# One attention-and-experts kernel: head sums in four column groups of TensorE, reciprocals laid as diagonal squares

## The chip, the cores and the metric

The kernel runs on one core of a Trainium2 chip. The metric is the device time of one execution in microseconds: the median of three runs is 970.37 us (966.24 to 972.15).

## The reference, cut to what matters

A layer on x of 4096 tokens by 512 channels, all in float32: linear attention with decay, a layer norm, a mixture of 64 experts with a shared one, a second layer norm. The change lies in the attention, and there in its denominator:

```python
qkv = x @ w_qkv                          # q, k, v: 16 heads of 32 channels
q, k = phi(q), phi(k)                    # phi(z) = elu(z) + 1
running_kv   = decay_scan(k * v)         # s_t = decay * s_{t-1} + x_t, per head
running_ksum = decay_scan(k)
den = clip(sum(q * running_ksum, over the 32 channels of a head), 1e-06)
out = q * running_kv / den               # den: one number per token and head
x1  = layernorm(x + out @ w_out)
```

## The kernel before, in words

**Tiling.** The tokens are cut into NB = 8 blocks of BT = 512, each into NJ = 4 tiles of 128. The channels are cut into KC = 4 chunks of 128, so a chunk holds 4 heads. In the attention, channels lie on the partitions and tokens run along the free axis. A step (it, c) projects chunk c of block it into k, v and q; there are 32 steps. To keep float32 accuracy at the higher rate, matmuls use float32r operands split into a high and a low part, three products each (`three`); an unsplit float32 matmul is recorded by the profiler as two weight loads and two matmuls.

**A step on each engine.** TensorE (`step` in the tensor block) projects k, v and q, twelve matmuls each, and between them it runs pieces of the block before, given by `mix(it, c, at)` for at = 0, 1, 2: head sums, the spreading of the reciprocals, and the rows of the output projection. ScalarE takes exp and relu of k and q out of PSUM. VectorE forms phi_k, scans it into run_k, multiplies by v into kv and scans that, forms phi_q, then qk = phi_q * run_k (one of five buffers), and one step later the numerator num = phi_q * run_kv. VectorE also splits, divides, adds the residual, takes norm statistics and routes tiles to experts.

**The denominator of a block** comes one block later, in the step c = 0:
- `sums(b, at)` on TensorE, at = 0 after the projection of k and at = 1 after that of v. For two of the four tiles each it multiplies the four chunks of qk, as the stationary operand (128 channels by 128 tokens), with `head_sum` (128 channels by 16 heads) and leaves 16 numbers per token, tokens on the partitions, in `small_ps`. The gate matmuls of the routing write into the same bank.
- `sums(b, at)` on VectorE clips them into `den` and writes the reciprocals twice into `rden`, at columns 0 and 32.
- `turn_rden(b)` on TensorE, after the projection of q: four transposes put heads on partitions and tokens along the free axis.
- `rden_high(b)` on ScalarE rounds the result to float32r, `rden_low(b)` on VectorE subtracts for the low part. Both lie in `rden_parts`, at partitions 0 to 15 and 32 to 47.
- `spread(b, part)` on TensorE, one matmul of 512 columns a chunk with `head_send` (ones where head and channel match), writes the reciprocal of every channel's head; `divide` on VectorE multiplies the numerator by it.

GpSimd builds the constants at the start (`head_sum`, `head_send` and the masks), each counted on the semaphore `consts`, and later computes the norms' scale and shift and issues the scatter of slots, one tile of six indirect DMAs a step.

**What sets the order.** All queues are written out by hand: `mix`, `sums_at`, `divide_at`, `out_at` and `tile_of` give the place of each piece, and every engine runs the same plan in order. A projection may overwrite one of three PSUM banks when the entry of `freed` says that its reader three projections before is through. After the eight blocks, the sums and the division of the last block stand in a stretch written out by itself, among the last tiles' norms, gates and counts and the first matmuls of the shared expert (`unit`):

```python
            count_rest(LAST - 5)
            sums(NB - 1, 0, LAST - 3)
            sums(NB - 1, 1, LAST - 3)
            count_before(LAST - 4)
            turn_x1(LAST - 3)
            gate(LAST - 3, 2 * NB)
            turn_rden(NB - 1)
            count_rest(LAST - 4)
            unit()
            spread(NB - 1, 0)
```

In the first block VectorE also splits the staged weights between its scans, so its queue there is longer than later. The experts follow when the table of slots is complete.

## Time and profile before

| | |
|---|---|
| median of three runs | 970.37 us (966.24 to 972.15) |
| profiled execution, span from first to last instruction | 967.4 us |
| profiled execution's own time beside its span | not listed apart |
| TensorE busy | 943.6 us, 98% |
| VectorE busy | 683.8 us, 71% |
| ScalarE busy | 502.8 us, 52% |
| GpSimd busy | 466.4 us, 48% |
| mean granted TensorE clock | 0.991 of full speed |

The attention part with its end lasts to about 490 us, the experts and the final norm fill the rest. PE is TensorE's matmuls, PEld its weight loads (they overlap), DVE VectorE, ACT ScalarE, POOL GpSimd. A busy matmul's end is modelled, and neighbours overlap; what a matmul costs is the distance to the next start. A line number is that of the helper that issues the instruction, so most matmuls show L1608 and are told apart by the names of their operands.

### The profile page before, as it was taken

To read this page: it belongs to the slowest core of one execution; us is meant where nothing else is said; L and a number is where in the kernel's file an instruction comes from. 1 tells how busy PE (TensorE), PEld (TensorE's weight loads), DVE (VectorE), ACT (ScalarE), POOL (GpSimd) and SP (SyncE) were. 2 spreads that over 40 slices of the span, in tenths; PEclk is the share of its full clock that TensorE was granted. 3 is DMA by queue.
4 is the path that set the end of the run, shared out by engine and by line. 5 is a ranking of instruction groups with operands and counts; after the bars stand their busy time and mean duration, and the time that the engine had idled before them with its cause. 6 is when DMAs were issued, how large, how long until landed. Compare 5 with 4: busy or idle time off the path is not lost. (4 is left out here: it accounts for less than half of the span.)

```text
span 967.4 us, 15236 instructions
## 1 busy us (share of the span) xinstructions
PE 943.6 (98%) x4658; PEld 757.0 (78%) x4658; DVE 683.8 (71%) x1251; ACT 502.8 (52%) x1015; POOL 466.4 (48%) x543
## 2 busy tenths in 40 slices
PE   8999999999999999999999999999999999999996
PEld 7888888888888888877887777777767777777875
DVE  7977786969778796887766565566565665636776
ACT  5532434434443443534447665566655665635775
POOL 4002264565556554587234544445545454432564
PEclk9999999999999999989999999999999999999999
DMA  6343452444252434346569999999999999979973
GB/s 202 96 145 109 144 125 91 131 114 132 80 167 91 119 109 140 103 152 231 171 195 272 292 323 307 310 318 294 327 319 316 308 318 298 320 135 372 373 268 118
DMA packets 114191, 203.93 MB, mean 211 GB/s; under 512 B 18496, under 2 KB 56384, under 8 KB 113088
## 3 DMA queue, kind: packets, MB, share of 16 engines
q1 hardware_dynamic: 93584, 159.87, 50.6%
q0 software_dynamic: 19520, 35.75, 16.3%
q10 hardware_dynamic: 1008, 7.34, 2.0%
q8 instruction: 39, 0.64, 0.3%
q14 instruction: 40, 0.33, 0.1%
HBM read 143.03 MB, written 59.88 MB: 210 GB/s over the span
## 5 line engine op out<-in xcount | busy, mean ns | idle before, releaser
L1511 POOL DMA_INDIRECT slot_table<-tokens,slot_of x162 | 179.2, 1106 | 112.0 <-issue 59.6
L1553 POOL DMA_INDIRECT acc_rows<-eo,table_sb x64 | 112.0, 1750 | 170.4 <-ACT eo L879 133.0
L1608 PE MATMUL bank<-x_hi,wqkv_hi 128*128 128x512 f32 x384 | 153.2, 399 | 1.4 <-DVE wqkv_lo L963 1.3
L1376 DVE TENSOR_TENSOR wgu_lo<-wgu,wgu_hi 128x1536 fp32r<-128x1536 f32 x64 | 112.4, 1758 | 55.0 <-ACT wgu_hi L873 55.0
L1608 PE MATMUL bank<-x_hi,wqkv_lo 128*128 128x512 f32 x384 | 150.8, 393 | 0.0
L1608 PE MATMUL bank<-x_lo,wqkv_hi 128*128 128x512 f32 x384 | 150.6, 392 | 0.0
L1608 PE MATMUL bank<-wdn,hid_et 96*128 96x512 f32 x256 | 122.1, 599 | 7.6 <-ACT hid_et L915 7.6
L873 ACT CAST wgu_hi<-wgu 128x1536 fp32r<-128x1536 f32 x64 | 94.5, 1477 | 12.5 <-DMA wgu<-w_gu 12.1
L1542 POOL DMA_INDIRECT xg<-x_rows,table_sb x64 | 74.9, 1170 | 42.0 <-DVE table_sb L1111 22.7
L1608 PE MATMUL bank<-wgu_hi,xgt_hi 128*128 128x384 f32 x256 | 91.6, 358 | 0.0
L647 ACT ACTIVATE e<-bank 128x512 f32<-128x512 f32 x64 | 38.0, 594 | 97.3 <-PE bank L1608 97.3
L1608 PE MATMUL bank<-wgu_hi,xgt_lo 128*128 128x384 f32 x256 | 86.0, 336 | 0.0
L1608 PE MATMUL bank<-wgu_lo,xgt_hi 128*128 128x384 f32 x256 | 85.9, 336 | 0.0
L1608 PEld LDWEIGHTS bank<-x_hi,wqkv_hi 128*128 128x128 f32 x384 | 72.7, 189 | 16.3 <-DVE wqkv_lo L963 2.0
L1608 PEld LDWEIGHTS bank<-x_hi,wqkv_lo 128*128 128x128 f32 x384 | 72.5, 189 | 16.0
L1608 PEld LDWEIGHTS bank<-x_lo,wqkv_hi 128*128 128x128 f32 x384 | 72.6, 189 | 14.8
L1608 PEld LDWEIGHTS bank<-wdn,hid_et 96*128 96x128 f32 x256 | 43.5, 190 | 40.2 <-issue 30.7
L1403 DVE SCALAR_TENSOR_TENSOR silu_e<-tanh_e,bank 128x192 f32<-128x192 f32 x64 | 22.6, 353 | 66.9 <-ACT tanh_e L903 66.7
L1495 POOL TENSOR_SCALAR rstd<-mv 128x1 f32<-128x1 f32 x32 | 9.2, 286 | 115.3 <-DVE mv L990 114.0
L879 ACT ACTIVATE eo<-bank,xg 128x512 f32<-128x512 f32 x64 | 44.3, 692 | 39.2 <-DMA acc_rows<-eo,table_sb 33.9
L1608 PE MATMUL bank<-wout_hi,att_hi 128*128 128x512 f32 x128 | 52.0, 407 | 1.7 <-issue 1.2
L903 ACT ACTIVATE tanh_e<-bank 128x192 f32<-128x192 f32 x64 | 21.2, 331 | 61.6 <-PE bank L1608 61.3
(179 smaller groups left out, 2211.6 us busy)
## 6 DMA issues: line engine op xcount, KB each, us to landing
wgu<-w_gu SPq DMA_DIRECT2D x64, 768.0 KB, 8.8
wdn<-w_down SPq DMA_DIRECT2D x64, 384.0 KB, 8.8
xres<-x SPq DMA_DIRECT2D x32, 256.0 KB, 3.2
x_turned<-x1t SPq DMA_DIRECT2D x32, 256.0 KB, 2.8
x_rows<-x SPq DMA_DIRECT2D x32, 256.0 KB, 3.1
acc_rows<-x SPq DMA_DIRECT2D x32, 256.0 KB, 3.1
fin<-acc_rows SPq DMA_DIRECT2D x8, 1024.0 KB, 12.1
odd<-acc_rows SPq DMA_DIRECT2D x8, 1024.0 KB, 13.5
```

The lines of the kernel that those rows point to most:

```text
L647: act.activation(e_sb[q][:, :], ps[:, :], ACT.Exp)
L873: act.copy(wgu_hi[e % 2][:, :, :], wgu_buf[e % NG][:, :, :]).then_inc(wgu_hi_done, 1)
L879: act.activation(eo[eo_slot[e]][:, :], eo_ps[:, :], ACT.Copy, scale=xg[e % NXG][:, D + e:D + e + 1]).then_inc(eo_done, 1)
L903: act.activation(tanh_e[:, :], gu_ps[e % 2][:, 0:I], ACT.Tanh, scale=0.5).then_inc(tanh_e_done, 1)
L1376: dve.tensor_tensor(wgu_lo[e % NG][:, :, :], wgu_buf[e % NG][:, :, :], wgu_hi[e % 2][:, :, :].bitcast(F32), ALU.subtract).then_inc(wgu_lo_ ...
L1403: dve.scalar_tensor_tensor(out=silu_e[:, :], in0=tanh_e[:, :], scalar=1.0, in1=ps[:, 0:I], op0=ALU.add, op1=ALU.mult).then_inc(silu_e_done, 1)
L1495: pool.tensor_scalar(rstd[i][:, :], mv[i][:, 1:2], EPS_NORM, None, ALU.add).then_inc(norm_done, 1)
L1511: pool.indirect_dma_start(table_dram, bass.IndirectOffsetOnAxis(slot_of[:, i, k:k + 1], 0), tokens[:, i:i + 1], None, bounds_check=SLOTS - ...
L1542: pool.indirect_dma_start(xg[e % NXG][:, :], None, x1_dram, bass.IndirectOffsetOnAxis(table_sb[:, e:e + 1], 0), bounds_check=T - 1, oob_is ...
L1553: pool.indirect_dma_start(acc_dram[e % 2], bass.IndirectOffsetOnAxis(table_sb[:, e:e + 1], 0), eo[eo_slot[e]][:, :], None, bounds_check=T ...
L1608: mm = pe.matmul(out_ap, a, b, start=first and i == 0, stop=final and i == len(products) - 1)
```

## The change

The head sums turn their operands round: `head_cols`, the head selector with every head's column written twice (32 columns), is stationary, and 128 tokens of qk stream through. Tile j writes to partitions 32j to 32j+31 of `small_ps`, which makes the matmul use column group j of the array. For a block that is 16 matmuls in one group, chunk outside and tile inside, all after the projection of k; the second place (at = 1) is gone. Heads now lie on partitions at once: lane 32j + 16r + h holds head h of tile j, r = 0 or 1 being two copies. So `turn_rden` and its semaphore are gone. VectorE clips and inverts 128 by 128 in one piece each. ScalarE rounds 128 by 128 to float32r (`rden_hi`). VectorE writes four squares of 32 lanes by 128 tokens along the diagonal of `rden_parts` with `low_mask` (0 for r = 0, -1 for r = 1): the first copy keeps the reciprocal, rounded, the second gets the reciprocal less its high part; the rest of `rden_parts` stays zero from the start. `head_send` is now filled over all 128 lanes. It is no longer built by GpSimd but by VectorE (`head_masks`, after the second step's scan), which picks each lane's head number and sign out of three small tables with the identity matrix. The diff, cut to its core:

```diff
@@ -111,7 +111,7 @@
-    head_sum = att.place("head_sum", [P, KC, HEADS])
+    head_cols = att.place("head_cols", [P, KC, 2, HEADS])
@@ -121,8 +121,11 @@
-    den = att.place("den", [P, NJ, HEADS])
-    rden = att.place("rden", [P, NJ, P // HALF, HALF])
+    den = att.place("den", [P, P])
+    rden = att.place("rden", [P, P])
+    rden_hi = att.place("rden_hi", [P, P], F32R)
+    low_mask = att.place("low_mask", [P, 1])
+    head_no = att.place("head_no", [P, 1])
@@ -156,6 +159,9 @@
+
+    col_head = qk[KC][:, :]
+    lane_head, lane_low, lane_junk = [num[KC + 1][:, i * P:(i + 1) * P] for i in range(3)]
@@ -258,7 +264,7 @@
-        return c == 0 and at < 2 and 0 <= it - 1 < NB
+        return c == 0 and at == 0 and 0 <= it - 1 < NB
...
@@ -692,10 +699,10 @@
                 act.copy(x1t_sb[i % 2][:, :, :], turn_ps[:, :].rearrange("p (k t) -> p k t", k=KC)).then_inc(x1t_done, 1)
             def rden_high(b):
-                act.wait_ge(rden_mm, b + 1)
+                act.wait_ge(rden_done, b + 1)
                 if b:
-                    act.wait_ge(send_mm, KC * b)
-                act.copy(rden_parts[:, :], send_ps[0][:, :]).then_inc(rden_hi_done, 1)
+                    act.wait_ge(rden_lo_done, NJ * b)
+                act.copy(rden_hi[:, :], rden[:, :]).then_inc(rden_hi_done, 1)
             def copy_logits(i):
                 act.wait_ge(score_mm, i + 1)
@@ -1026,28 +1033,37 @@
                 dve.wait_ge(x1_added, i + 1)
                 norm(i, x1_sb[slot][:, :])
-            def sums(b, at):
-                n = 2 * b + at
-                cols = slice(at * NJ // 2 * HEADS, (at + 1) * NJ // 2 * HEADS)
-                tiles = slice(at * NJ // 2, (at + 1) * NJ // 2)
-                dve.wait_ge(heads_mm, n + 1)
+            def sums(b):
+                dve.wait_ge(heads_mm, b + 1)
                 if b:
-                    dve.wait_ge(rden_done, n - 1)
-                dve.tensor_scalar(den[:, tiles, :].rearrange("p j h -> p (j h)"), small_ps[:, cols], EPS_DEN, None,
-                                  ALU.max).then_inc(den_clipped, 1)
-                dve.wait_ge(den_clipped, n + 1)
-                dve.wait_ge(consts, C_SEND)
+                    dve.wait_ge(rden_done, b)
+                dve.tensor_scalar(den[:, :], small_ps[:, 0:P], EPS_DEN, None, ALU.max).then_inc(den_clipped, 1)
+                dve.wait_ge(den_clipped, b + 1)
                 if b:
-                    dve.wait_ge(rden_mm, b)
-                dve.reciprocal(rden[:, tiles, 0:2, 0:HEADS],
-                               den[:, tiles, :].unsqueeze(2).to_broadcast([P, NJ // 2, 2, HEADS])).then_inc(rden_done, 1)
+                    dve.wait_ge(rden_hi_done, b)
+                    dve.wait_ge(rden_lo_done, NJ * b)
+                dve.reciprocal(rden[:, :], den[:, :]).then_inc(rden_done, 1)
             def rden_low(b):
                 dve.wait_ge(rden_hi_done, b + 1)
+                dve.wait_ge(low_mask_done, 1)
                 if b:
                     dve.wait_ge(send_mm, KC * b)
-                low = rden_parts[HALF:HALF + HEADS, :]
-                dve.tensor_tensor(low, send_ps[0][HALF:HALF + HEADS, :], low.bitcast(F32), ALU.subtract).then_inc(rden_lo_done, 1)
+                for j in range(NJ):
+                    of = slice(j * HALF, (j + 1) * HALF)
+                    dve.scalar_tensor_tensor(out=rden_parts[of, j * P:(j + 1) * P], in0=rden_hi[of, :].bitcast(F32),
+                                             scalar=low_mask[of, 0:1], in1=rden[of, :], op0=ALU.mult,
+                                             op1=ALU.add).then_inc(rden_lo_done, 1)
+
+            def head_masks():
+                dve.wait_ge(consts, C_LANES)
+                dve.scalar_tensor_tensor(out=lane_junk, in0=ident[:, :], scalar=1.0, in1=lane_head, op0=ALU.mult, op1=ALU.mult,
+                                         accum_out=head_no[:, :]).then_inc(head_no_done, 1)
+                dve.wait_ge(head_no_done, 1)
+                dve.scalar_tensor_tensor(out=lane_junk, in0=ident[:, :], scalar=1.0, in1=lane_low, op0=ALU.mult, op1=ALU.mult,
+                                         accum_out=low_mask[:, :]).then_inc(low_mask_done, 1)
+                dve.tensor_scalar(head_send[:, :, :].rearrange("p k c -> p (k c)"), col_head, head_no[:, 0:1], None,
+                                  ALU.is_equal).then_inc(head_send_done, 1)
             def top(i):
                 dve.wait_ge(logits_done, i + 1)
@@ -1277,6 +1291,10 @@
                                        op0=ALU.mult, op1=ALU.add).then_inc(run_kv_done, 1)
                 if s == 0:
                     x_low(1, 0)
+                if s == 1:
+                    head_masks()
+                if s == len(qk) - 1:
+                    dve.wait_ge(head_send_done, 1)
                 mix(it, c, 1)
                 if (it, c) == (NB - 1, KC - 1):
                     dve.wait_ge(shared_hi_done, 2)
@@ -1455,27 +1471,19 @@
             pool.tensor_scalar(expert_no[:, :], expert_no[:, :], -1.0 / P, None, ALU.mult).then_inc(consts, 1)
             pool.memset(big_no[:, :], float(BIG // P)).then_inc(consts, 1)
-            pool.memset(head_sum[:, :, :], 1.0).then_inc(consts, 1)
+            pool.memset(head_cols[:, :, :, :], 1.0).then_inc(consts, 1)
             for n, (sign, base) in enumerate(((1, 0), (-1, HW - 1))):
                 pool.wait_ge(consts, C_SUM - 2 + n)
-                pool.affine_select(out=head_sum[:, :, :], in_=head_sum[:, :, :], compare_op=ALU.is_ge, fill=0.0, base=base,
-                                   pattern=[[sign * HW * per_chunk, KC], [-sign * HW, HEADS]],
+                pool.affine_select(out=head_cols[:, :, :, :], in_=head_cols[:, :, :, :], compare_op=ALU.is_ge, fill=0.0, base=base,
+                                   pattern=[[sign * HW * per_chunk, KC], [0, 2], [-sign * HW, HEADS]],
                                    channel_multiplier=sign).then_inc(consts, 1)
-            pool.memset(rden[:, :, :, :], 0.0).then_inc(consts, 1)
-            mask_f = kv[:, :].rearrange("p (k c) -> p k c", k=KC)
-            pool.memset(mask_f, 0.0).then_inc(consts, 1)
-            pool.wait_ge(consts, C_SUM + 2)
-            halves = [mask_f[0:HEADS], mask_f[HALF:HALF + HEADS]]
-            for mask in halves:
-                pool.memset(mask, 1.0).then_inc(consts, 1)
-            for n, (sign, base) in enumerate(((1, 0), (-1, HW - 1))):
-                pool.wait_ge(consts, C_SUM + 4 + 2 * n)
-                for mask in halves:
-                    pool.affine_select(out=mask, in_=mask, compare_op=ALU.is_ge, fill=0.0, base=base,
-                                       pattern=[[sign * HW * per_chunk, KC], [sign, P]],
-                                       channel_multiplier=-sign * HW).then_inc(consts, 1)
-            pool.wait_ge(consts, C_SEND - 1)
-            pool.tensor_copy(head_send[:, :, :], mask_f).then_inc(consts, 1)
+            pool.memset(rden_parts[:, :].bitcast(F32), 0.0).then_inc(consts, 1)
+            pool.iota(col_head.rearrange("p (k h w) -> p k h w", k=KC, h=per_chunk), pattern=[[per_chunk, KC], [1, per_chunk], [0, HW]],
+                      base=0, channel_multiplier=0, allow_small_or_imprecise_dtypes=True).then_inc(consts, 1)
+            pool.iota(lane_head.rearrange("p (r h) -> p r h", h=HEADS), pattern=[[0, P // HEADS], [1, HEADS]], base=0,
+                      channel_multiplier=0, allow_small_or_imprecise_dtypes=True).then_inc(consts, 1)
+            pool.iota(lane_low.rearrange("p (j r h) -> p j r h", j=NJ, r=2), pattern=[[0, NJ], [-1, 2], [0, HEADS]], base=0,
+                      channel_multiplier=0, allow_small_or_imprecise_dtypes=True).then_inc(consts, 1)
             pool.memset(minus_half[:, :], -0.5).then_inc(consts, 1)
             pool.iota(tokens[:, :], pattern=[[P, NT]], base=0, channel_multiplier=1).then_inc(consts, 1)
             pool.iota(table_sb[:, :], pattern=[[0, E]], base=T, channel_multiplier=0).then_inc(consts, 1)
@@ -1625,8 +1633,11 @@
             def spread(b, part):
                 n = b * KC + part
-                pe.wait_ge(consts, C_SEND)
-                pe.wait_ge(rden_lo_done, b + 1)
+                pe.wait_ge(consts, C_LANES)
+                pe.wait_ge(head_send_done, 1)
+                pe.wait_ge(rden_lo_done, NJ * (b + 1))
+                if part == 0 and b:
+                    pe.wait_ge(div_done, KC * b)
                 if part == 1 and b:
                     pe.wait_ge(x1_added, NJ * b)
                 if part >= 2:
@@ -1647,29 +1658,20 @@
                                first=k == 0, final=k == KC - 1)
                 mm.then_inc(out_mm, 1)
-            def sums(b, at, gated):
+            def sums(b, gated):
                 pe.wait_ge(consts, C_SUM)
                 pe.wait_ge(qk_done, KC * (b + 1))
-                if at and b < NB - 1:
-                    pe.wait_ge(den_clipped, 2 * b + 1)
-                elif gated:
+                if gated:
                     pe.wait_ge(logits_done, gated)
                 elif b:
-                    pe.wait_ge(den_clipped, 2 * b)
-                for j in range(at * NJ // 2, (at + 1) * NJ // 2):
-                    mm = chain(small_ps[:, j * HEADS:(j + 1) * HEADS],
-                               [(qk[(b * KC + k) % len(qk)][:, j * P:(j + 1) * P], head_sum[:, k, :]) for k in range(KC)])
+                    pe.wait_ge(den_clipped, b)
+                for k in range(KC):
+                    heads = head_cols[:, k, :, :].rearrange("p r h -> p (r h)")
+                    for j in range(NJ):
+                        mm = pe.matmul(small_ps[j * HALF:(j + 1) * HALF, 0:P], heads, qk[(b * KC + k) % len(qk)][:, j * P:(j + 1) * P],
+                                       start=k == 0, stop=k == KC - 1)
                 mm.then_inc(heads_mm, 1)
-
-            def turn_rden(b):
-                pe.wait_ge(rden_done, 2 * b + 2)
-                pe.wait_ge(consts, C_IDENT)
-                if b:
-                    pe.wait_ge(div_done, KC * b)
-                for j in range(NJ):
-                    mm = pe.transpose(send_ps[0][:, j * P:(j + 1) * P], rden[:, j, :, :].rearrange("p r h -> p (r h)"), ident[:, :])
-                mm.then_inc(rden_mm, 1)
             def count_before(i):
                 pe.wait_ge(any_done, i + 1)
@@ -1778,12 +1780,10 @@
-                if c == 0 and it:
-                    turn_rden(it - 1)
-                    gate(tile, 2 * it if c == 0 else 0)
+                    gate(tile, it if c == 0 else 0)
@@ -1797,12 +1797,10 @@
-            sums(NB - 1, 0, LAST - 3)
-            sums(NB - 1, 1, LAST - 3)
+            sums(NB - 1, LAST - 3)
-            gate(LAST - 3, 2 * NB)
-            turn_rden(NB - 1)
+            gate(LAST - 3, NB)

```

Left out are the semaphores' names and counts, which follow.

## Rows read from the trace of the kernel before

**Rows 1.** The page: the span, and busy time, share and instructions of each engine.

```profile
span 967.4 us, 15236 instructions
PE 943.6 (98%) x4658; PEld 757.0 (78%) x4658; DVE 683.8 (71%) x1251; ACT 502.8 (52%) x1015; POOL 466.4 (48%) x543
```

**Rows 2.** TensorE's waits, 50 to 440 us: total, times, longest.

```profile
PE bank L1709 <- ACT x L668: 0.8, 1, 0.8
PE bank L1608 <- ACT x1t L692: 0.7, 1, 0.7
```

**Rows 3.** Busy time in three stretches; PEclk is the granted clock.

```profile
20.00:44.00 24.00, 23.84 (x106) 19.41 (x104) 23.79 (x35) 13.00 (x31) 0.00 (x0) 1.00 0.44 127
...
50.00:440.00 390.00, 388.26 (x2014) 321.87 (x2013) 308.72 (x634) 164.69 (x417) 200.49 (x231) 0.99 0.42 124
...
429.00:435.00 6.00, 5.33 (x23) 4.67 (x24) 3.61 (x9) 2.24 (x5) 5.02 (x5) 0.50 0.91 314
```

**Rows 4.** Groups of instructions: busy us, mean ns | idle before.

```profile
L1608 PE MATMUL bank<-head_sum,qk 128*128 128x16 f32 x256 | 30.1, 260 | 0.3 <-DVE qk L1294 0.3
...
L1403 DVE SCALAR_TENSOR_TENSOR silu_e<-tanh_e,bank 128x192 f32<-128x192 f32 x64 | 22.6, 353 | 66.9 <-ACT tanh_e L903 66.7
```

**Rows 5.** Timeline of TensorE, it = 2, c = 0: start, duration.

```profile
96.51 1.85 PE L1608 MATMUL bank<-head_sum,qk 128*128 128x16 f32 x16
98.21 0.49 PE L1608 MATMUL bank<-x_hi,wqkv_hi 128*128 128x512 f32 x1
...
101.51 1.86 PE L1608 MATMUL bank<-head_sum,qk 128*128 128x16 f32 x16
103.22 0.48 PE L1608 MATMUL bank<-x_hi,wqkv_hi 128*128 128x512 f32 x1
...
106.06 0.60 PE L1671 MATMUL bank<-ident,rden 128*128 128x128 f32 x4
106.50 0.19 PE L1680 MATMUL bank<-big_no,ones 128*128 128x64 bf16 x1
```

**Rows 6.** Timeline of TensorE in the expert part.

```profile
781.92 1.89 PE L1608 MATMUL bank<-wdn,hid_et 96*128 96x512 f32 x4
783.64 0.38 PE L1884 MATMUL bank<-ident,hid_e 128*96 128x128 f32 x2
```

**Rows 7.** Timeline of VectorE, it = 3, c = 0; idle before in brackets.

```profile
153.83 0.18 DVE L1036 TENSOR_SCALAR den<-bank 128x32 f32<-128x32 f32 x1
154.05 0.55 DVE L1042 RECIPROCAL rden<-den 128x64 f32<-128x64 f32 x1
...
162.50 0.69 DVE L1288 SCALAR_TENSOR_TENSOR phi_q<-e,relu 128x512 f32<-128x512 f32 x1 [3.21 <-ACT relu L652]
...
163.95 0.68 DVE L1050 TENSOR_TENSOR rden_parts<-bank,rden_parts 16x512 fp32r<-16x512 f32 x1
```

**Rows 8.** Timeline of TensorE at the first head sums.

```profile
43.22 0.39 PE L1608 MATMUL bank<-x_lo,wqkv_hi 128*128 128x512 f32 x1
43.45 0.39 PE L1608 MATMUL bank<-x_hi,wqkv_lo 128*128 128x512 f32 x1
44.19 1.93 PE L1608 MATMUL bank<-head_sum,qk 128*128 128x16 f32 x16 [0.35 <-DVE qk L1294]
```

**Rows 9.** Timeline of four engines after the last block.

```profile
425.36 4.02 PE L1608 MATMUL bank<-head_sum,qk 128*128 128x16 f32 x32
...
428.17 0.23 DVE L1068 TENSOR_TENSOR any_choice<-logits,replaced 128x64 bf16<-128x64 f32 x1
...
430.04 0.18 DVE L1036 TENSOR_SCALAR den<-bank 128x32 f32<-128x32 f32 x1
...
454.87 0.27 POOL L1499 TENSOR_SCALAR shift<-mv,rstd 128x1 f32<-128x1 f32 x1
...
455.90 0.80 ACT L668 ACTIVATE x<-x,shift,rstd 128x512 f32<-128x512 f32 x1
...
457.17 0.64 PE L1709 MATMUL bank<-ident,x 128*128 128x128 f32 x4
```

More of the change, by code:

```diff
@@ L364, in build @@
             sem("phi_q_done"), sem("qk_done"), sem("den_clipped"), sem("rden_done"), sem("rden_lo_done"))
+        low_mask_done, head_no_done, head_send_done = sem("low_mask_done"), sem("head_no_done"), sem("head_send_done")
         div_done, att_lo_done, x1_added, stats_done, mv_done = (
@@ L375, in build @@
         last_applied = sem("last_applied")
-        k_mm, v_mm, q_mm, heads_mm, rden_mm, send_mm, out_mm = (
-            sem("k_mm"), sem("v_mm"), sem("q_mm"), sem("heads_mm"), sem("rden_mm"), sem("send_mm"), sem("out_mm"))
+        k_mm, v_mm, q_mm, heads_mm, send_mm, out_mm = (
+            sem("k_mm"), sem("v_mm"), sem("q_mm"), sem("heads_mm"), sem("send_mm"), sem("out_mm"))
         turn_mm, score_mm, before_mm, rest_mm = sem("turn_mm"), sem("score_mm"), sem("before_mm"), sem("rest_mm")
@@ L381, in build @@
         xgt_mm, gu_mm, ht_mm, eo_mm = sem("xgt_mm"), sem("gu_mm"), sem("ht_mm"), sem("eo_mm")
-        C_IDENT, C_BEFORE, C_SUM, C_SEND, C_HALF, C_TOKEN, C_TABLE, C_ZEROS, C_PADS, C_HOT = 2, 10, 13, 22, 23, 24, 25, 26, 27, 29
+        C_IDENT, C_BEFORE, C_SUM, C_LANES, C_HALF, C_TOKEN, C_TABLE, C_ZEROS, C_PADS, C_HOT = 2, 10, 13, 17, 18, 19, 20, 21, 22, 24
         freed = []
@@ L762, in unit @@
                     if b == 0 and j == 0:
-                        act.wait_ge(heads_mm, 2 * NB)
+                        act.wait_ge(heads_mm, NB)
                     if b == 1 and j == 0:
@@ L1140, in mix @@
                 if sums_at(it, c, at):
-                    sums(it - 1, at)
+                    sums(it - 1)
             def split_x1t(b):
@@ L1268, in step @@
                     dve.wait_ge(run_kv_done, s)
-                else:
-                    dve.wait_ge(consts, C_SEND)
                 dve.tensor_tensor(kv[:, :], phi_k[:, :], proj_ps[1][:, :], ALU.mult).then_inc(kv_done, 1)
@@ L1292, in step @@
                 if s >= len(qk):
-                    dve.wait_ge(heads_mm, 2 * ((s - len(qk)) // KC) + 2)
+                    dve.wait_ge(heads_mm, (s - len(qk)) // KC + 1)
                 dve.tensor_tensor(qk[s % len(qk)][:, :], phi_q[:, :], run_k[:, :], ALU.mult).then_inc(qk_done, 1)
@@ L1325, in _ @@
             split_shared(su_hi, su_lo, su_stage)
-            dve.wait_ge(heads_mm, 2 * NB)
-            sums(NB - 1, 0)
-            sums(NB - 1, 1)
+            sums(NB - 1)
             place(LAST - 4)
@@ L1730, in mix @@
                     gated = tile_of(it, -1)
-                    sums(it - 1, at, 0 if gated is None else gated + 1)
+                    sums(it - 1, 0 if gated is None else gated + 1)
             unit_at = [0]
```

## The prediction

> **What bounds the kernel now.** I start with busy times: TensorE is busy 943.6 of a span of 967.4 us [rows 1]. A busy TensorE can still be a waiting one, so next come its waits in the stretch in which the change lies, 50 to 440 us: the two longest are 0.8 and 0.7 us [rows 2]. Between 50 and 440 us VectorE is busy 308.7 of 390 us and ScalarE 164.7 [rows 3]. So in the attention part TensorE sets the pace, and an instruction taken from it shortens the kernel by its spacing to the next one, not by its recorded duration: the records overlap. Two places are different. Between 20 and 44 us VectorE is busy 23.79 of 24 us [rows 3], and TensorE then waits 0.35 us for its last qk product [rows 8]: there VectorE is the pace. And just after the last block (425 to 457 us) TensorE, VectorE and GpSimd are all close to late [rows 9]. The expert part that follows starts from what the attention part leaves; nothing in it is tied to an absolute time, so a gain ahead of it moves it as a whole.
>
> **What is removed on TensorE.** Head sums: per block two groups of 16 records (a float32 matmul is recorded as two; 256 records in all, [rows 4]). The first takes from 96.51 to 98.21 us, the second from 101.51 to 103.22 [rows 5]: 1.70 + 1.71 = 3.41 us, or 0.106 us a record. The streamed operand has only 16 columns, so this 0.106 us is the price of loading 128 stationary columns, not of streaming. The four transposes of the reciprocals take from 106.06 to 106.50: 0.44 us [rows 5]. Together 3.85 us a block, and 7 of the 8 blocks lie in the stretch that TensorE paces: 27.0 us to be had there at most.
>
> **What is added on TensorE.** Again 16 float32 matmuls a block, so 32 records, but with 32 stationary columns and 128 streamed. Streaming price: four float32 records of 512 columns take from 781.92 to 783.64, 0.43 us each [rows 6], so 128 columns cost 0.108 us. Loading price: a quarter of 0.106, 0.027 us. One after the other with the loads hidden, 32 records take 3.44 us: **the same as now**. The whole gain hangs on whether matmuls in different column groups run at the same time, and no row of this trace has two matmuls side by side. The bounds are therefore 8 slots of 0.108 (all four groups always full, 0.86 us) and 32 times 0.108 + 0.027 with nothing hidden (4.32 us). Between them: both records of one matmul go to the same column group, so the second must wait for the first; only the second record of one and the first of the next are free to overlap. That makes 16 slots of 0.108, 1.72 us. I take this value: it needs the groups to be independent but keeps the order of the records, as every row of TensorE has it. Changing shape twice costs something: a 512-column float32r record lasts 0.39 us and the next one comes 0.23 later [rows 8], and if the 0.16 us of overlap is lost at entry and exit that is 0.3 us a block (lower bound 0, upper also the 0.3, since an entry to the small group already exists now). So 2.0 us a block, against 3.85 now: 1.85 saved, times 7 = **13.0 us**.
>
> The Trainium skill ("TensorE: Matmul & The Clock Gate", Part 3, the table of measured speedups) gives 2.38 times for three column tiles of 32; by it the 3.44 us would become an estimated 1.45 us and the gain 16.8 us. Three tiles at once need more overlap than the pairs I count, and no row here shows either.
>
> **VectorE per block.** Removed: two clips (0.18 each), two reciprocals of 64 columns (0.55 each), one subtraction of 0.68 [rows 7]. Added: a clip of 128 columns (about 0.28), a reciprocal of 128 (1.08), four masked sums of 32 partitions by 128 columns; the nearest row is 0.35 us for 192 columns [rows 4], so about 0.27 each, 1.1 in all, with 0.7 and 1.4 as ends. Net +0.3 us. The clip and reciprocal now both stand ahead of the scan of k, 0.6 us later than now, and behind it the product with v and its scan. The cover is the 3.21 us for which VectorE sits idle in that step before phi_q [rows 7]. With TensorE 1.4 us earlier at that point, 3.21 - 1.4 = 1.8 us are left and the 0.6 fits in: no cost. With the groups always full TensorE comes 2.25 us earlier, and 0.96 - 0.6 is still positive. ScalarE's cast shrinks from 512 to 128 columns, off the path. Nothing queues behind the four masked sums but the placing of a tile, which has the same idle time as cover.
>
> **Start.** GpSimd's constants change, and no wait on them ended late. But VectorE gets three new instructions after its second step: two masked sums of 128 columns and a comparison of 512 (about 0.27, 0.27 and 0.65: 1.2 us; ends 0.9 and 1.5). VectorE has no idle time from there to 44 us [rows 3], so the last qk of block 0 is 1.2 us late, and TensorE waits at the first head sums for it [rows 8]. **1.2 us lost.**
>
> **The last block.** Its sums fill 425.36 to 429.2, then comes a count that needs any_choice, written at 428.17 [rows 9]. With sums of 2.0 us TensorE reaches the count at 427.4 and waits a microsecond for it. Then the gate matmul needs the clip of the sums, which VectorE starts at 430.04, behind a long split; that does not move. From 429 to 435 the granted clock is 0.50, that is 1.2 GHz [rows 3], after nearly 4 us of records of 16 streamed columns; if it does not fall then, a further 2 us come back. But GpSimd works without a pause through this stretch and gives the shift of the tile LAST at 454.87 + 0.27 = 455.14, ScalarE takes 0.8 us for it, so 455.95 is the earliest for the transpose that now starts at 457.17 [rows 9]. Whatever is gained above, **1.2 us** of it come out.
>
> **Sum.** -13.0 + 1.2 - 1.2 = -13.0 us. The span is 967.4 us; the profiled execution's time is not listed by itself, and the median of the three runs, 970.4, stands 3.0 above the span. I subtract from the median: 957.4 us.
>
> **The rivals.**
> *Four groups always full* (the loads and both records find a free group). 1.16 us a block, 2.69 saved, times 7: -18.8 us, 951.6. For it: a stationary operand of 32 columns can be in place early. Against it: consecutive records of one matmul share a group.
> *No overlap at all: the change does not do what its name says.* 3.44 + 0.3 us a block, 0.11 saved times 7, the ends cancel nearly (-0.9 + 1.2): 969.9. For it: a streamed float32 operand already costs twice what a float32r one costs per column (0.43 against 0.23 us, [rows 6, 8]), so the reading side may be what is full.
> *Slower: the small stationary loads are not hidden.* Now loads run beside the matmul before. If with column groups each load waits until the group ahead is through, a block costs 32 x (0.108 + 0.027) + 0.3 = 4.6 us, 0.8 more than now, times 7 = 5.6, plus the start 1.2, less some 0.3 in the last block: +6.5 us, 976.9. It decides from the point where a record with its load takes over 3.85 / 32 = 0.120 us. For it: the present sums are already paced by their loads. Against it: in every row a load for the next matmul goes ahead. If each record of 0.26 us [rows 4] even had to end before the next starts, it would be 32 x 0.26 + 0.3 - 3.85 = 4.8 us a block and 33 us in all; I give that 3 in 100.
> The Trainium skill has the rule behind this rival ("TensorE: Matmul & The Clock Gate", Part 3, The mechanism): a weight load overlaps running matmuls only where the row group differs, and here all four tiles use all rows. "TensorEngine Tiling (Array Packing)", Key Properties, adds that a change of tiling mode drains the engine. No row here shows either.
>
> **Chances.** Paired overlap 0.40, four groups full 0.25, no overlap 0.17, loads exposed 0.18 (with the 0.03). The likeliest gives 957.4. The range goes from 949 (four groups full, with a microsecond for the unknown clock at 46 and 429 us on either side) to 971 (no overlap); it leaves out the exposed loads. The likeliest case alone would be 953 to 961. About 1% (9.7 us) is what a measurement of this kernel can tell from no change. Faster by more: all of the second case, nearly all of the first less a part for noise, 0.60. Slower by more: only when a record with its load costs above 0.15 us, 0.08. Within 1%: 0.32.
>
> **What would show it.** Each block's head sums as one group of 32 records, its length from first start to the next matmul's start: about 2.0 us (paired), 1.2 (full), 3.7 (none), 4.6 or more (loads exposed). No transposes of rden. TensorE's wait for qk at 44 us grown from 0.35 to about 1.5 us. VectorE still idle before phi_q in each first step. A new wait of TensorE for any_choice in the last block, and its transpose of tile LAST behind ScalarE. The prediction fails if the groups don't overlap, or if VectorE's wait before phi_q has gone and TensorE waits for kv instead.

## The result, and the profile after

The changed kernel takes **954.1 us** (median of 6 runs, 948.4 to 956.6), the kernel before 970.3 in its 6 runs beside it. The ratio is 0.984, 95% interval 0.9815 to 0.9868: faster by 1.6%. The forecast was 957.4 us with a range of 949 to 971, faster. Total, sign and range came out right, but the total by luck: the term behind most of it was wrong by 6.9 us, and a wait that the text had excluded paid nearly all of that back.

The page of the changed kernel, span and busy times (beside [rows 1]). The profiled execution took 948.4 us, 1.8 more than its span:

```profile
span 946.6 us, 15180 instructions
PE 919.8 (97%) x4626; PEld 728.2 (77%) x4626; DVE 686.2 (72%) x1264; ACT 500.1 (53%) x1015; POOL 466.0 (49%) x538
```

The span is 20.8 us shorter and TensorE's busy time 23.8. Busy time alone says neither where nor why. Its windows come next (columns as in [rows 3]):

```profile
20.00:44.00 24.00, 23.52 (x104) 19.14 (x102) 23.75 (x38) 11.89 (x29) 0.00 (x0) 1.00 0.41 124
44.00:50.00 6.00, 5.30 (x51) 4.39 (x52) 5.96 (x10) 2.01 (x4) 0.00 (x0) 1.00 0.32 86
50.00:440.00 390.00, 380.55 (x2029) 305.23 (x2028) 322.73 (x675) 168.69 (x433) 213.58 (x245) 0.99 0.44 134
412.00:420.00 8.00, 5.48 (x20) 4.63 (x21) 7.16 (x24) 3.88 (x9) 6.47 (x6) 0.61 0.82 264
```

TensorE, busy 388.26 of 390 us in the middle stretch before, is now idle for 9.5 us of it. TensorE's waits from 50 to 440 us name the new idle time (total, times, longest; beside [rows 2]):

```profile
PE bank L1645 <- DVE rden_parts L1054: 4.1, 7, 1.4
PE bank L1684 <- DVE any_choice L1084: 1.9, 1, 1.9
PE bank L1711 <- ACT x L675: 1.2, 1, 1.2
```

For rden_parts TensorE waited only once before, for 0.23 us. The wait for ScalarE's x stood there too (0.8 us, [rows 2]), and the one for any_choice belongs to the last block. TensorE's timeline, at the first head sums, in it = 3, and after the last block (beside [rows 5, 8, 9]):

```profile
44.70 1.08 PE L1672 MATMUL bank<-qk,head_cols 128*32 128x128 f32 x32 [1.18 <-DVE qk L1312]
...
146.53 1.08 PE L1672 MATMUL bank<-qk,head_cols 128*32 128x128 f32 x32
147.54 0.50 PE L1616 MATMUL bank<-x_hi,wqkv_hi 128*128 128x512 f32 x1
...
157.22 0.39 PE L1616 MATMUL bank<-x_hi,wqkv_lo 128*128 128x512 f32 x1
158.06 0.47 PE L1645 MATMUL bank<-rden_parts,head_send 128*128 128x512 f32 x1 [0.46 <-DVE rden_parts L1054]
158.37 0.39 PE L1616 MATMUL bank<-x_hi,wqkv_hi 128*128 128x512 f32 x1
...
410.69 1.08 PE L1672 MATMUL bank<-qk,head_cols 128*32 128x128 f32 x32
...
413.68 0.23 PE L1684 MATMUL bank<-any_choice,before 128*128 128x64 bf16 x1 [1.91 <-DVE any_choice L1084]
...
441.56 0.64 PE L1711 MATMUL bank<-ident,x 128*128 128x128 f32 x4
...
481.27 0.60 PE L1842 MATMUL bank<-ident,xg 128*128 128x128 f32 x4
```

The 32 records of a block last from 146.53 to 147.54: **1.01 us**, where two groups of 1.7 us stood, and the transposes of rden are gone. That is the rival "four groups always full", not the forecast's pairs.

**Where the gain lies.** Three marks divide every profile of this case: the start of the first head sums, the start of the last ones, and the start of the expert part's first transposes (xg).

```
                        first sums  last sums  first xg   span   loop   tail   rest
before                       44.19     425.36    496.98  967.4  381.2   71.6  470.4
before, another profile      44.03     425.20    496.73  969.4  381.2   71.5  472.7
after                        44.70     410.69    481.27  946.6  366.0   70.6  465.3
after, another               43.95     410.02    481.55  952.1  366.1   71.5  470.6
after, a third               44.75     410.76    480.83  947.4  366.0   70.1  466.6
```

Loop is the time from the first to the last sums, tail from there to xg, rest from there to the end. The loop repeats within 0.1 us and is **15.2 us** shorter. The start is 0.4 us later (means of the profiles), the tail 0 to 1.5 shorter. The rest is code that the change doesn't touch, and it varies by 5 us from one profile to the next of the same kernel. A part of that is the clock: the granted clock falls to 0.50 in both profiles of before at 725 us, for 3.4 and 6.8 us, and in the second of after at 572 us for 6.8; the first and the third of after have none in the rest until its last 5 us, where every profile of the two kernels has one. Of the 20.8 us between the two profiled spans 5.1 lie in the rest; whether any of them are a gain of the change is not shown.

### The profile page after: what moved, and what is told of

Its sections match the earlier page's. It is cut to its first block and busy times, and to the rows that moved or that the text cites. A ratio compares the mean times of both kernels' runs of the same rounds, so it can differ in the third digit from the quotient of the medians.

```text
span 946.6 us, 15180 instructions
## 1 busy us (share of the span) xinstructions
PE 919.8 (97%) x4626; PEld 728.2 (77%) x4626; DVE 686.2 (72%) x1264; ACT 500.1 (53%) x1015; POOL 466.0 (49%) x538
## 5 line engine op out<-in xcount | busy, mean ns | idle before, releaser
L1519 POOL DMA_INDIRECT slot_table<-tokens,slot_of x162 | 181.5, 1120 | 95.4 <-issue 50.0
L1550 POOL DMA_INDIRECT xg<-x_rows,table_sb x64 | 79.8, 1247 | 42.0 <-DVE table_sb L1127 22.7
```

The costliest lines, as they stand in the source:

```text
L1519: pool.indirect_dma_start(table_dram, bass.IndirectOffsetOnAxis(slot_of[:, i, k:k + 1], 0), tokens[:, i:i + 1], None, bounds_check=SLOTS - ...
L1550: pool.indirect_dma_start(xg[e % NXG][:, :], None, x1_dram, bass.IndirectOffsetOnAxis(table_sb[:, e:e + 1], 0), bounds_check=T - 1, oob_is ...
```

## The experiments

In all ratios below the kernel before ran beside on the same chip.

**The changed kernel again** (labels after_again and, later, after_third), without an edit, as the measure for the others.

> The changed kernel itself, unedited, as the reference for the runs beside it. Theory (side by side): its 32 records of head sums take 1.0 us a block because the four column groups run at once, TensorE waits about 0.46 us a block for rden_parts. Both again here; time 0.984 of the kernel before, about 954 us. Theory (luck of the clock): a good part of the profile's 20.8 us was two falls of the clock fewer, and its attention part (first head sums to the experts' first transposes) is only some 16 us shorter; then the 16 us repeat here and what lies behind the experts' start varies by a few us.

> The changed kernel unedited, as the reference beside the run before: 0.980 to 0.984 of the kernel before; first to last head sums 366 us, the stretch to the experts' first transposes 70.6 to 71.5 us, the rest anywhere between 465 and 473 us.

Measured: 952.95 us, 0.9804 [0.9773, 0.9835], and 951.0 us, 0.9809 [0.978, 0.9838], as expected. With the first measurement, gains of 16.2, 18.0 and 18.1 us. The wait for rden_parts is 4.1 us in all three profiles.

**The low part ahead of phi_q** (early_low). ScalarE's rounding and VectorE's four masked sums are each issued earlier in the step, so that the sums fall into VectorE's idle time before phi_q:

```diff
+                if c == 0 and it:
+                    rden_high(it - 1)      # ScalarE: ahead of copy_turned(tile)
...
-                if c == 0 and it:
-                    rden_high(it - 1)
@@ VectorE
+                if c == 0 and it:
+                    rden_low(it - 1)       # before phi_q
...
-                if c == 0 and it:
-                    rden_low(it - 1)       # was behind the qk product
```

> Rounding of the reciprocals moved ahead of the copy of the turned tile on ScalarE, the four masked sums moved ahead of phi_q on VectorE, into its idle time of 2.0 us. Theory (the low part is late): the wait before the first spread (4.1 us in seven blocks) and the 0.08 us of lost overlap behind each of them go: 4 to 5 us faster than the changed kernel, ratio to it 0.995 to 0.996, period of a block 53.07 -> 52.5 us. Rival (VectorE is the pace by now): the masked sums delay phi_q and the wait turns up at another place; no gain, 53.07 stays.

Measured: 946.3 us, 0.9758 [0.9731, 0.9785], beside 0.9804 for the changed kernel: 6.7 us less by the medians, where 4 to 5 were expected. VectorE and TensorE of the changed kernel in it = 3:

```profile
155.01 0.69 DVE L1306 SCALAR_TENSOR_TENSOR phi_q<-e,relu 128x512 f32<-128x512 f32 x1 [2.01 <-ACT relu L659]
155.73 0.69 DVE L1312 TENSOR_TENSOR qk<-phi_q,run_k 128x512 f32<-128x512 f32 x1
156.34 1.46 DVE L1054 SCALAR_TENSOR_TENSOR rden_parts<-rden_hi,low_mask,rden 32x128 fp32r<-32x128 f32 x4
```

and of this experiment, VectorE and then TensorE:

```profile
150.25 1.50 DVE L1054 SCALAR_TENSOR_TENSOR rden_parts<-rden_hi,low_mask,rden 32x128 fp32r<-32x128 f32 x4
152.33 0.69 DVE L1308 SCALAR_TENSOR_TENSOR phi_q<-e,relu 128x512 f32<-128x512 f32 x1 [0.58 <-ACT relu L659]
```

```profile
143.85 1.08 PE L1672 MATMUL bank<-qk,head_cols 128*32 128x128 f32 x32
...
154.77 0.39 PE L1645 MATMUL bank<-rden_parts,head_send 128*128 128x512 f32 x1
```

VectorE's idle time before phi_q goes from 2.01 to 0.58 us: the masked sums have moved into it. From phi_q to the spread there are now 2.44 us instead of 3.05, and the wait is gone in every block. The loop is 358.8 us, 7.2 less. The late low parts thus cost 7.2 us, while the list of waits shows 4.1. A steady block is 0.87 us shorter for a recorded wait of 0.46, and the starts show where the remainder is. From 157.22 to the spread at 158.06 are 0.84 us, where 0.23 is usual: 0.61 lost, for a matmul's recorded 0.39 us hide the first part of a wait. The next matmul then comes after 0.31 in place of 0.23. And at the block's first output matmul (234.48 us in the block from 199.60) another 0.16 us go, which no list of waits names; it reads what the divisions behind the spreads produce.

**The head masks first** (masks_first). GpSimd makes the three small tables ahead of its other constants, and VectorE builds the masks before its loop, not behind the second step:

```diff
-                if s == 1:
-                    head_masks()
...
+            head_masks()                   # ahead of the loop; the tables' counts follow
```

> GpSimd fills the three small tables first, and VectorE builds the head masks before its first subtraction (it is idle there until 4.2 us) and not behind the second step. Theory (VectorE paces the first block): the first head sums start 0.8 us earlier, at about 43.9 us, and TensorE's wait for qk falls from 1.18 to about 0.4 us; kernel 0.8 us faster, within noise. Rival (the 1.2 us are hidden elsewhere): 44.7 us stays, or the start moves later by what the constants now delay.

Measured: 949.9 us, 0.9796 [0.9768, 0.9824]: not to be told from the changed kernel (0.9804). TensorE at the first sums:

```profile
43.48 1.08 PE L1671 MATMUL bank<-qk,head_cols 128*32 128x128 f32 x32 [0.86 <-DVE qk L1310]
```

The first sums start 1.2 us earlier than in the first profile after, 0.5 than in the second; expected were 0.8. The start itself moves by 0.8 us among profiles of one kernel, so an effect of this size is bounded, not measured.

**Both edits together** (both, and again as both_again beside clip_first).

> The two edits before together. Theory: 5 to 6 us faster than the changed kernel, ratio to it 0.994 to 0.995, about 948.5 us, and faster than either alone. Rival: no more than the changed kernel.

> The version of both edits unedited, as the reference beside the run before. Both theories: 0.9735 of the kernel before, the stretch from the last head sums to the experts' first transposes about 71 us.

Measured: 944.0 us, 0.9735 [0.9707, 0.9764], and 949.6 us, 0.9795 [0.9756, 0.9833]. The first is 9.0 us below the changed kernel, where 5 to 6 were expected, but not to be told from the low part alone (0.9758); the second misses the 0.9735 that was expected to repeat. Loop 358.8 us again. In the second profile the rest is 473.1 us, against 467.2 in the first: the difference between the two measurements lies where no edit is.

**One column group for all** (one_group). All four tiles write to partitions 0 to 31, side by side, so all 32 records use column group 0. The sizes of loads, records and streamed columns stay the same; the addition over the four chunks is left out:

```diff
+            dve.memset(small_ps[:, :], 1.0)
...
-                        mm = pe.matmul(small_ps[j * HALF:(j + 1) * HALF, 0:P], heads, ...
-                                       start=k == 0, stop=k == KC - 1)
+                        mm = pe.matmul(small_ps[0:HALF, j * P:(j + 1) * P], heads, ...
+                                       start=True, stop=True)
```

> The changed kernel with all 16 head-sum matmuls of a block in column group 0: tile j writes to partitions 0 to 31, columns 128j on, in place of partitions 32j on, columns 0 on. Same instructions, same operands, same order. The sums over the four chunks are left out (each matmul overwrites), and lanes 32 to 127 of the denominator are a constant, so the attention output is not the reference's. Theory (groups run side by side): the overlap goes, 32 x 0.108 = 3.4 us a block in place of 1.0, 2.4 us more times 7: +17 us on the changed kernel less what its wait for rden_parts now hides (nothing: the sums lie ahead of the clip), so about 969, the time of the kernel before. Rival (the gain comes from loading 32 stationary columns and not 128, whatever the group): 1.0 us a block stays and the time too.

**The tile outside, the chunk inside** (tile_outer): the four groups as in the changed kernel, but eight records in a row to each.

```diff
-                for k in range(KC):
-                    heads = head_cols[:, k, :, :].rearrange("p r h -> p (r h)")
-                    for j in range(NJ):
+                for j in range(NJ):
+                    for k in range(KC):
+                        heads = head_cols[:, k, :, :].rearrange("p r h -> p (r h)")
```

> The changed kernel with the two loops of its head sums exchanged: tile outside, chunk inside, so 8 records in a row go to one column group before the next. Result unchanged. Theory (a record waits at the head of the queue until its own group is free, few may pass): 8 x 0.108 = 0.86 us for each group, little overlap between groups: 3 to 3.4 us a block, kernel +14 to +17 us on the changed one. Rival (each group has its own queue, deep enough to let all four start): 1.0 us a block, no change. My paired-overlap forecast assumed the first even for two records.

**Half the streamed columns** (half_stream): 64 tokens of each tile instead of 128, in the changed kernel's order; the other half is left out.

```diff
+            dve.memset(small_ps[:, :], 1.0)
...
-   mm = pe.matmul(small_ps[j * HALF:(j + 1) * HALF, 0:P], heads, qk[...][:, j * P:(j + 1) * P],
+   mm = pe.matmul(small_ps[j * HALF:(j + 1) * HALF, 0:P // 2], heads, qk[...][:, j * P:j * P + P // 2],
```

> The changed kernel with 64 streamed columns in each head-sum matmul in place of 128: half of the tokens' sums are left out (a constant stands there). Theory (streaming paces, four groups full: 8 x 0.108 = 0.86 us and a tail): 8 x 0.054 = 0.43 us and the tail, 0.6 us a block; kernel 2 to 3 us faster than the changed one. Rival (the start of records or the loads of 32 columns pace, 0.032 us each): 1.0 us a block stays.

Measured: one_group 969.3 us, 1.0009 [0.9985, 1.0033]; tile_outer 962.5, 0.9932 [0.9908, 0.9956]; half_stream 950.2, 0.9822 [0.9769, 0.9875]. TensorE in the same block of each: the sums, and the matmul behind them. First one_group:

```profile
151.60 3.68 PE L1673 MATMUL bank<-qk,head_cols 128*32 128x128 f32 x32
155.21 0.50 PE L1617 MATMUL bank<-x_hi,wqkv_hi 128*128 128x512 f32 x1
```

tile_outer:

```profile
149.06 2.46 PE L1672 MATMUL bank<-qk,head_cols 128*32 128x128 f32 x32
151.45 0.50 PE L1616 MATMUL bank<-x_hi,wqkv_hi 128*128 128x512 f32 x1
```

half_stream:

```profile
146.28 0.65 PE L1673 MATMUL bank<-qk,head_cols 128*32 128x64 f32 x32
146.87 0.50 PE L1617 MATMUL bank<-x_hi,wqkv_hi 128*128 128x512 f32 x1
```

From the sums' start to the next matmul's 3.61, 2.39 and 0.59 us, beside 1.01 in the changed kernel. Expected were 3.4 for one_group and 0.6 for half_stream; for tile_outer neither theory held, the one with 3 to 3.4 us nor the one with 1.0. The distance from one block's sums to the next (mean of five blocks) follows almost one for one: 55.64, 54.43, 52.63 and 53.05 us. (half_stream's loop is 2.6 us shorter than the changed kernel's, but its total, 0.9822, doesn't show it; its rest took 469.4 us.) So three things are told apart. Without the column groups the whole gain is gone. one_group also drops the addition over chunks, but that is not what slows it: tile_outer keeps it, and its records within one group stand 0.109 us apart as well. A column group can't be changed here without the partitions of `small_ps` that it writes, so the two stay one cause. Having the groups is not enough: the order in which the records reach them is worth 1.4 us a block. And with the loads the same, half the columns take 0.42 us less: the streaming paces the sums, not the loads.

**The clip ahead of the split** (clip_first, clip_first_2): both edits, and in the last block VectorE takes the clip and reciprocal, and places tile LAST - 4, before it makes the low part of the shared up weights. In the kernel before that piece stands just ahead of the clip, which starts at 430.04 [rows 9]:

```profile
428.39 1.74 DVE L1231 TENSOR_TENSOR su_lo<-su_stage,su_hi 128x1536 fp32r<-128x1536 f32 x1
```

```diff
-            split_shared(su_hi, su_lo, su_stage)
             ...                            # the last block's sums(NB - 1)
+            split_shared(su_hi, su_lo, su_stage)
```

> The version of both edits, and after the last block VectorE clips and inverts the head sums and places tile LAST - 4 before it makes the low part of the shared up weights (1.7 us), not after it. Theory (GpSimd's scatters cap the stretch after the last block, as I forecast): TensorE's wait for the clip (1.3 us) goes and the division may start up to 1.7 us earlier, but the transpose of tile LAST stays held by the shift that GpSimd gives behind its scatters, and at most 0.5 us come out: ratio to the unedited version 0.9995 to 1.000, last head sums to the experts' first transposes 71 us as now. Rival (VectorE's order is what holds the stretch): 1.3 to 1.7 us faster, 69.7 us for that stretch.

> The version with all three moves (low part early, head masks first, clip ahead of the split) once more, beside the changed kernel. From the traces: seven blocks 7.2 us shorter, first head sums 0.5 to 1 us earlier, the stretch after the last block 0.4 to 1.4 us shorter: 8 to 10 us faster than the changed kernel, ratio to it about 0.9905.

Measured: 945.6 us, 0.9762 [0.9726, 0.9798], beside 0.9795 for both_again; and 944.2 us, 0.9741 [0.9721, 0.9762], beside 0.9809 for the changed kernel. ScalarE, GpSimd and TensorE of clip_first in the tail:

```profile
432.70 0.81 ACT L675 ACTIVATE x<-x,shift,rstd 128x512 f32<-128x512 f32 x1 [1.71 <-POOL shift L1505]
```

```profile
432.40 0.27 POOL L1505 TENSOR_SCALAR shift<-mv,rstd 128x1 f32<-128x1 f32 x1
```

```profile
433.57 0.66 PE L1709 MATMUL bank<-ident,x 128*128 128x128 f32 x4 [1.24 <-ACT x L675]
```

TensorE's wait for den (1.3 us in both) is gone in the two profiles. Here it waits 1.24 us for ScalarE instead, which waited 1.71 us for GpSimd. But one_group, which doesn't have this edit, shows the same two waits:

```profile
458.31 0.81 ACT L675 ACTIVATE x<-x,shift,rstd 128x512 f32<-128x512 f32 x1 [1.71 <-POOL shift L1508]
```

```profile
459.18 0.66 PE L1712 MATMUL bank<-ident,x 128*128 128x128 f32 x4 [1.24 <-ACT x L675]
```

So does tile_outer (1.73 and 1.25). What differs is the clock. Over the 30 us from 5 before the last sums on, the mean granted clock is 0.89 in nine of the fourteen profiles, with tails of 70.5 to 71.7 us; 0.94 in three (clip_first, masks_first, after_third), with 69.9 to 70.2; and 1.00 in one_group and tile_outer, with 69.7 and 69.4. clip_first_2, at 0.89 again, has 0.45 us of ScalarE's wait for GpSimd and none of TensorE's. The tail is 70.2 and 70.5 us, against 71.2 and 71.1 for both and 70.6 for the first profile of the changed kernel: what the edit itself gives is below 1 us and not told apart. GpSimd is the limit where the clock holds. clip_first_2 is 6.8 us (0.7%) faster than the changed kernel beside it, where 8 to 10 were expected; its step past "both" is not told apart by the times.

**The kernel before, once more** (before_look), for its clock at the first sums.

> The kernel before, one more profile. Theory (its first head sums bring the clock down): the granted clock falls to 0.5 for some 3 us behind the first head sums, as it did at 46.3 us in the trace shown, which costs 1.7 us and would be part of the gain. Rival (chance of that one execution): no fall there, and first to last head sums 379.5 us in place of 381.2.

Measured: 971.2 us (one execution). The fall that was expected is there, and the loop is 381.2 us again. Its window and TensorE's records, at the place where the changed kernel has a granted clock of 1.00:

```profile
44.00:50.00 6.00, 5.97 (x27) 5.15 (x28) 4.64 (x8) 1.34 (x3) 0.00 (x0) 0.72 0.41 121
```

```profile
47.19 0.63 PE L1608 MATMUL bank<-x_hi,wqkv_hi 128*128 128x512 f32 x1
47.61 0.63 PE L1608 MATMUL bank<-x_lo,wqkv_hi 128*128 128x512 f32 x1
```

## Why the prediction came out right, step by step

**The head sums: mis-sized.** The step that failed reads "only the second record of one and the first of the next are free to overlap", which made 16 slots of 0.108 us and, with 0.3 for the edges, 2.0 us a block. The single records of the changed kernel start four at a time, 7 ns one after the other, and the next four 0.109 us later (0.133 after the first round). Eight rounds make 0.87 us, and with 0.14 more, most of it behind the last round, it is 1.01 us to the next matmul. In one_group and tile_outer two records of one group never start closer than 0.109 us, so the four that start within 20 ns are in four groups, and belong to four matmuls. I had put each second record between two matmuls, as if it held up the next one; here the four groups run abreast. (Which of a matmul's two records is which the trace doesn't say.) In tile_outer, where the order really gives one group eight records in a row, at most two groups overlap, and only for a part of their records: 2.39 us, nearer to my 2.0. The sums and transposes together save 3.85 - 1.01 = 2.84 us a block, **19.9 us** in seven, not 13.0. The 0.108 us per 128 columns, taken from 512-column records, was right, and so was 0.3 for the edges as an upper bound.

**Loads exposed, or no overlap: neither.** The 32-column loads are recorded at 106 to 110 ns each, the 128-column ones before at 188 to 192; my price was a quarter. They add nothing: 32 of them lie within 1.01 us, and within 0.59 in half_stream. The rule named with that rival in the forecast (the Trainium skill, "TensorE: Matmul & The Clock Gate", Part 3, The mechanism: a load overlaps running matmuls only where the row group differs) doesn't agree: all four tiles use all rows here, and all loads ran beside matmuls. The measurement decides. The table in the same part of the Trainium skill gives 2.38 times for three column tiles; one_group against the changed kernel is 3.61 / 1.01 = 3.6 times for four.

**VectorE: a wait missed.** I wrote that "Nothing queues behind the four masked sums but the placing of a tile". On VectorE that is so, but TensorE's first spread waits for them. The trace of before had what was needed. Its spreads in it = 1, where TensorE waits for them already, and in it = 3, beside [rows 7]:

```profile
58.56 0.47 PE L1634 MATMUL bank<-rden_parts,head_send 128*128 128x512 f32 x1 [0.23 <-DVE rden_parts L1050]
...
165.38 0.39 PE L1634 MATMUL bank<-rden_parts,head_send 128*128 128x512 f32 x1
```

In it = 3 the single subtraction ended at 163.95 + 0.68 = 164.63, so the margin was 0.75 us. Taking away the transposes, which TensorE runs between the projection that phi_q comes from and this spread, uses 0.44 of it. The other 0.31 is less than the 0.42 by which even my own price (1.1 for 0.68) lengthened this link. With the measured 1.46 us for the four, 342 ns each against my 0.27, the link is 0.78 longer and the wait 0.46. Idle time ahead of phi_q was no cover, for the sums stood behind phi_q. There was more of it than I had reckoned, 2.01 us and not 0.96 - 0.6: VectorE's two shorter waits ahead of it in the trace of before (0.60 and 0.20 us) shrink first, and of the two pairs of clip and reciprocal the second, 0.73 us, falls away. early_low puts the whole cost at 7.2 us. Of that 0.5 were there before, in it = 1 (start to start), so 6.7 are the change's: 19.9 - 6.7 = 13.2, by chance my 13.0. The clip (0.28) came out as priced and the reciprocal a little shorter (0.95 against 1.08); that pair cost nothing.

**The start: 0.4 us lost, not 1.2.** VectorE in the changed kernel:

```profile
26.19 0.27 DVE L1060 SCALAR_TENSOR_TENSOR num<-ident,num 128x128 f32<-128x128 f32 x1
...
26.72 0.48 DVE L1065 TENSOR_SCALAR head_send<-qk,head_no 128x512 fp32r<-128x512 f32 x1
27.12 0.69 DVE L1306 SCALAR_TENSOR_TENSOR phi_q<-e,relu 128x512 f32<-128x512 f32 x1
```

The masks take 27.12 - 26.19 = 0.93 us. TensorE's wait for qk grew from 0.35 to 1.18, by 0.83, but the sums start only 0.4 later on the mean; the marks of one kernel differ by more than that.

**The last block: 0 to 1.5 us.** As forecast, TensorE waits for any_choice (1.91 us), then for den (0.83). The granted clock still falls to 1.2 GHz there (0.61 from 412 to 420), so those 2 us did not come back. The sign "its transpose of tile LAST behind ScalarE" did not come: at 441.56 TensorE doesn't wait, and ScalarE had taken the tile at 440.29, when GpSimd's shift was ready for 0.8 us (439.24 + 0.27). So it was not GpSimd that capped the gain in this profile. That cap is real, but shows only where the clock falls less or not at all, as in one_group: there the tail is 1.9 us shorter than before.

**Not foreseen: the first block's clock.** In both profiles of before the granted clock falls to 0.5 behind the first sums, after a short wait and 1.8 us of 16-column records:

```profile
46.50:49.50 3.00, 3.00 (x8) 2.35 (x8) 2.31 (x4) 0.00 (x0) 0.00 (x0) 0.50 0.57 164
```

Ten 512-column records then take from 45.97 to 49.93, 3.96 us, where the same ten take 2.41 in the changed kernel: 1.55 lost, with the sums' own 0.08 some 1.6. In the changed kernel and in all the experiments with 32-column loads the window from 44 to 50 us has 1.00. That the change prevents the fall is read from two profiles against twelve; why, was not tried. I had expected some of this at the last block and not at the first.

**The sum, as measured.** Loop: -19.9 + 6.7 - 1.6 = -14.8, of -15.2; 0.4 stays unnamed. The loop's 15.2 with the start (+0.4) and tail (0 to -1.5) make 14.8 to 16.3 us. The medians say 16.2, 18.0 and 18.1. The missing part, up to 3 us, would have to lie in the expert part, which varies by more; whether the change shifts something in it, no run here settles.

## What to carry to other kernels

If a matmul has few stationary columns, put independent outputs in different column groups and issue them in turn, one to each group, so that several groups run abreast; eight in a row to one group give up more than half of the gain. Before giving a result to more and shorter instructions on another engine, take the margin of its reader from the trace (end of the producer, start of the reader) and shorten it by what the change takes out of the reader's own engine. Short instructions don't scale down with their columns: a masked sum of 128 columns took 0.34 us where the one subtraction of 512 took 0.68, so four pieces cost 1.46. And read what a wait costs from start to start: the recorded idle time of 0.46 us stood for 0.70 at the spread.

## What was not expected of the hardware

- Records to four column groups start 7 ns one after the other, four within 20 ns. With 128 streamed float32 columns the next round comes 0.109 us later, with 64 columns 0.056.
- With eight records in a row to one group, the next group's first record starts while three of the first group's are still to come, 0.467 us behind it; hence 2.39 us, between 3.61 and 1.01.
- In one_group and tile_outer the granted clock stays at 1.00 from 405 to 440 us, and on to the experts' first transposes; in both profiles of before and in two of three of the changed kernel it is 0.90 there, in the third 0.95. In one_group and tile_outer the sums are longer and the waits behind them differ; which of these holds the clock was not tried.
